# Attention megakernel on one core: first two units load their queries once and copy them on chip, and the weights are quantised in the bias stage

## The reference, cut to what matters

```python
q = heads(x @ Wq + bq); k = heads(x @ Wk + bk); v = heads(x @ Wv + bv)      # 48 x 1024 x 16
attn = einsum('bqd,bkd->bqk', q, k) / sqrt(HD)
rel_bias_h = einsum('bhwc,hkc->bhwk', rq, Rh)                                # q times a table of rows
rel_bias_w = einsum('bhwc,wkc->bhwk', rq, Rw)                                # q times a table of columns
attn = softmax(attn + rel_bias_h[..., None] + rel_bias_w[..., None, :])
x = x + einsum('bqk,bkd->bqd', attn, v) @ Wp + bp
wq1 = round(clip(w1 / alpha_w1, -8, 7)); wq2 = round(clip(w2 / alpha_w2, -8, 7))
x = x + ffn(layernorm(x), wq1, wq2)
```

## Time and profile before

| | us |
|---|---|
| median of 3 runs | 881.89 |
| lowest, highest | 879.38, 884.87 |
| the profiled execution | 880.72 |
| its span (first to last instruction of the program) | 878.9 |
| projection stage | 0 to 101.8 |
| bias stage | 101.8 to 159.4 |
| attention stage | 159.4 to about 762 |
| feed-forward stage | to 878.9 |

### The profile page before, as it was taken

The page is one execution under the profiler, slowest core; times in us unless marked ns, Lnnn a source line. Parts: engine busy times, 40 slices in busy tenths (PEclk is TensorE's granted clock), DMA queues, the critical chain, the costliest instruction groups (busy, mean ns, idle before and its releaser), DMA issues. The chain is left out here.

```text
span 878.9 us, 14775 instructions
## 1 busy us (share of the span) xinstructions
PE 775.8 (88%) x5656; PEld 404.5 (46%) x5656; DVE 696.7 (79%) x965; ACT 574.0 (65%) x969; POOL 447.7 (51%) x284
## 2 busy tenths in 40 slices
PE   4999456588999999999999999999999998678874
PEld 2655456243444444444444444444444441356653
DVE  6998844696888888888888888888888880179995
ACT  1343335136787778787878777787777878257673
POOL 3677796445373738474665748373734444012120
PEclk9999767679999999999999999999999999889986
DMA  7675599999977584939293949577690001333411
GB/s 195 214 223 192 177 286 363 311 184 184 155 151 163 123 186 95 203 76 213 69 209 68 222 82 201 107 158 151 132 178 13 13 1 34 116 132 102 145 37 54
DMA packets 65750, 130.02 MB, mean 148 GB/s; under 512 B 9535, under 2 KB 45392, under 8 KB 57224
## 3 DMA queue, kind: packets, MB, share of 16 engines
q1 hardware_dynamic: 57648, 115.95, 57.1%
q10 hardware_dynamic: 8032, 13.13, 4.3%
HBM read 89.73 MB, written 34.60 MB: 141 GB/s over the span
## 5 line engine op out<-in xcount | busy, mean ns | idle before, releaser
L1031 DVE TENSOR_REDUCE at_neg_max<-at_r_ps 128x1 f16<-128x1024 f32 x384 | 451.7, 1218 | 86.4 <-PE at_r_ps L903 86.4
L989 ACT ACTIVATE at_probs<-at_s_ps 128x512 f32<-128x512 f32 x768 | 410.8, 600 | 97.4 <-PE at_s_ps L923 96.5
L923 PE MATMUL at_s_ps<-op_mix_q,op_mix_k 128*128 128x512 f16 x768 | 264.3, 383 | 10.8 <-issue 3.9
L903 PE MATMUL at_r_ps<-op_mix_k,op_mix_q 128*128 128x256 f16 (+1 forms) x1920 | 239.9, 258 | 13.3 <-DMA op_mix_q<-bias_parts 8.6
L935 PE MATMUL at_o_ps<-at_probs,op_v_u 128*32 128x512 f32 x1536 | 204.1, 604 | 0.0
L903 PEld LDWEIGHTS at_r_ps<-op_mix_k,op_mix_q 128*128 128x128 f16 x1920 | 157.3, 100 | 91.3 <-DVE at_neg_max L1031 15.7
L822 POOL COPY op_mix_q<-op_mix_q 2x4096 f16<-2x4096 f16 x48 | 171.6, 3601 | 1.5
L923 PEld LDWEIGHTS at_s_ps<-op_mix_q,op_mix_k 128*128 128x128 f16 x768 | 73.8, 97 | 175.5 <-issue 74.4
L220 POOL MEMSET op_mix_q<- 2x10240 f32 x12 | 103.5, 8628 | 21.2 <-PE at_o_ps L935 21.1
L826 POOL TENSOR_TENSOR at_o_sb<-at_o_sb,at_inv_rows 128x512 f32<-128x512 f32 x24 | 30.7, 1279 | 141.1 <-DVE at_inv_rows L1047 139.9
L819 POOL COPY op_mix_q<-op_mix_q 2x1024 f16<-2x1024 f16 x24 | 24.9, 1036 | 113.0 <-ACT op_mix_q L994 113.0
(11 more groups left out here) (116 smaller groups left out, 655.2 us busy)
## 6 DMA issues: line engine op xcount, KB each, us to landing
op_mix_q<-qk_parts SPq DMA_DIRECT2D x48, 640.0 KB, 10.7
op_mix_q<-bias_parts SPq DMA_DIRECT2D x120, 120.0 KB, 9.6
op_mix_q<-bias_parts SPq DMA_DIRECT2D x72, 128.0 KB, 9.5
qk_parts<-op_mix_q SPq DMA_DIRECT2D x24, 256.0 KB, 2.4
v_rows<-pr_v_st SPq DMA_DIRECT2D x8, 768.0 KB, 4.1
op_mix_k<-qk_parts SPq DMA_DIRECT2D x48, 128.0 KB, 13.2
op_v_u<-v_rows SPq DMA_DIRECT2D x12, 512.0 KB, 13.9
op_mix_q<-bias_parts SPq DMA_DIRECT2D x24, 256.0 KB, 9.9
```

Of the source, the lines that this page charges most:

```text
L903: last = pe.matmul(r_ps[count % RRING][:, first // GROUP, first % GROUP:first % GROUP + n], mix_q[owner.buf][:, variant, j, qt * P:(qt + 1 ...
L923: pe.matmul(s_ps[use % SRING][:, :], mix_k[unit.buf][:, j, keys], mix_q[unit.buf][:, ops.VARIANT_OF[kt], j, queries], start=True, stop=Tru ...
L989: act.activation(probs[n % PRING][:, j, :], s_ps[use % SRING][:, :], ACT.Exp).then_inc(s_taken, 1)
L1031: dve.tensor_reduce(neg_max[half][:, j // 2, t, j % 2:j % 2 + 1], r_ps[count % RRING][:, :, :].rearrange("p h t -> p (h t)"), AX_X, ALU.ma ...
```

## The change

Four edits.

1. Units 0 and 1 load their queries into variant 0 alone (`load_first_q`, 4 DMAs of 128 KB each, with a semaphore `q_in` of their own). Variants 1 to 4 are made by copies of 64 partitions x 4096 float16. For unit 0 DVE makes them in the bias stage, two after item 3 and two after item 4. For unit 1 ACT makes two and POOL makes two at the start of the attention stage. All later units load as before (`load_q`).
2. The weights are quantised by DVE in the bias stage, w1 after item 0 and w2 after item 1.
3. SP asks for unit 0's first loads without waiting for `tab_lo`; the waits for `tab_lo` and for the quantised weights now stand ahead of `load_bias`.
4. POOL turns the queries half by half over the images, and PE waits for a half instead of the whole.

```diff
-        for r, part in enumerate((0, 0, 1, 1)):
-            src = q_or_k(0, part).unsqueeze(1).to_broadcast([HD, self.VARIANTS, QUAD * SEQ])
...
+    def load_first_q(self, sp, i):
+
+        for r, part in enumerate((0, 0, 1, 1)):
+            sp.dma_start(self.mix_q[i][r:self.A_AT:4, 0, :, :].rearrange("p j t -> p (j t)"), self.q_or_k(0, i, 0, part)).then_inc(self.q_in[i], 16)
+
+    def variant_of_q(self, i, variant):
+        return self.mix_q[i][0:self.A_AT, variant, :, :].rearrange("p j t -> p (j t)")
...
-                if g.last:
-                    prepare.quantise(dve, 0)
-                    prepare.quantise(dve, 1)
...
+    QUANTISE_AFTER, SPREAD_AFTER = (0, 1), {3: (1, 2), 4: (3, 4)}
...
-                for image in range(BATCH):
-                    for half in range(2):
+                for half in range(2):
+                    for image in range(BATCH):
...
-            sp.wait_ge(tables.tab_lo, 2 * CHUNKS)
-            ops.load_qkv(sp, 0, 0)
-            ops.load_hot(sp, hot_a, hot_b, parity)
+            ops.load_first_q(sp, 0)
+            ops.load_kv(sp, 0, 0)
+            ops.load_hot(sp, hot_a, hot_b, parity)
+            sp.wait_ge(prepare.quantised, 2)
+            sp.wait_ge(tables.tab_lo, 2 * CHUNKS)
...
-                if t == 1:
-                    pe.wait_ge(q_turned, (quad + 1) * 2 * BATCH)
+                    if t == 1 and ch * PER % BLK == 0:
+                        pe.wait_ge(q_turned, (quad * 2 + ch * PER // BLK + 1) * BATCH)
...
+                if i in QUANTISE_AFTER:
+                    prep.quantise(dve, QUANTISE_AFTER.index(i))
+                if i in SPREAD_AFTER:
+                    dve.wait_ge(ops.q_in[0], 16 * 4)
+                    dve.wait_ge(prep.quantised, 2)
+                    dve.wait_ge(tables.tab_lo, 2 * CHUNKS)
+                    for variant in SPREAD_AFTER[i]:
+                        dve.tensor_copy(ops.variant_of_q(0, variant), ops.variant_of_q(0, 0)).then_inc(ops.q_spread[0], 1)
...
+            pool.wait_ge(ops.q_in[1], 16 * 4)
+            for variant in Q_BY_POOL:
+                pool.tensor_copy(ops.variant_of_q(1, variant), ops.variant_of_q(1, 0)).then_inc(ops.q_spread[1], 1)
...
+            act.wait_ge(ops.q_in[1], 16 * 4)
+            for variant in Q_BY_ACT:
+                act.activation(ops.variant_of_q(1, variant), ops.variant_of_q(1, 0), ACT.Copy).then_inc(ops.q_spread[1], 1)
```

More of the change, by code:

```diff
@@ L155, in __init__ @@
         self.loaded = [self.sem(f"loaded{i}") for i in range(3)]
+        self.q_in, self.q_spread = ([self.sem(f"{n}{i}") for i in range(2)] for n in ("q_in", "q_spread"))
         early, late = (m[:, :, :, :].rearrange("p v j t -> p (v j t)") for m in self.mix_q[1:])
@@ L220, in zero_max, with load_kv, loads_of, q_or_k @@
         pool.memset(rows, 0.0).then_inc(self.max_zeroed, 1)
[L222 to L227, removed]
-        for r, part in enumerate((0, 0, 1, 1)):
-            src = q_or_k(0, part).unsqueeze(1).to_broadcast([HD, self.VARIANTS, QUAD * SEQ])
-            sp.dma_start(self.mix_q[i][r:self.A_AT:4, :, :, :].rearrange("p v j t -> p v (j t)"), src).then_inc(self.loaded[i], 16)
+    def load_kv(self, sp, image, i):
         for r, part in enumerate((0, 1, 0, 1)):
-            sp.dma_start(self.mix_k[i][r:self.A_AT:4, :, :].rearrange("p j t -> p (j t)"), q_or_k(1, part)).then_inc(self.loaded[i], 16)
+            sp.dma_start(self.mix_k[i][r:self.A_AT:4, :, :].rearrange("p j t -> p (j t)"), self.q_or_k(image, i, 1, part)).then_inc(self.loaded[i], 16)
         sp.dma_start(self.v_u[i][:, :, :, :].rearrange("p k h e -> p k (h e)"),
                      self.v_dram[bass.ds(image, 1), :, :, i * QUAD * SLOT:(i + 1) * QUAD * SLOT].rearrange("b p k e -> (b p) k e")).then_inc(self.loaded[i], 16)
+    def loads_of(self, buf, images):
+        return 16 * (self.N_LOADS * images - (4 if buf < 2 else 0))
+    def load_first_q(self, sp, i):
[3 more added lines that the diff above has]
+        return self.mix_q[i][0:self.A_AT, variant, :, :].rearrange("p j t -> p (j t)")
+    def q_or_k(self, image, i, which, part):
+        chunk, half = ((which, i), (2, which))[i == 2]
+        src = self.qk_dram[bass.ds(image, 1), chunk, part, half * QC:(half + 1) * QC, :]
+        return src.rearrange("b (d j) t -> (b d) (j t)", d=HD)
+    def load_q(self, sp, image, i):
+        for r, part in enumerate((0, 0, 1, 1)):
+            src = self.q_or_k(image, i, 0, part).unsqueeze(1).to_broadcast([HD, self.VARIANTS, QUAD * SEQ])
+            sp.dma_start(self.mix_q[i][r:self.A_AT:4, :, :, :].rearrange("p v j t -> p v (j t)"), src).then_inc(self.loaded[i], 16)
     def load_bias(self, sp, u, i):
@@ L738, in phase_attention @@
     SRING, RRING = 3, 2
+    Q_BY_ACT, Q_BY_POOL = (1, 2), (3, 4)
     with Phase(nc, "at") as ph:
@@ L741, in phase_attention @@
         MAX_ROW, TILE_ORDER = ops.MAX_ROW, ops.TILE_ORDER
[L742 removed]
+        consts, loaded = ops.consts, ops.loaded
         neg_max = [ph.sb(f"neg_max{h}", [P, QUAD // 2, TILES, 2], F16) for h in range(2)]
@@ L863, in _ @@
             ops.copy_hot(sp)
-            ops.load_qkv(sp, 0, 1)
+            ops.load_first_q(sp, 1)
+            ops.load_kv(sp, 0, 1)
             sp.wait_ge(ops.bias_stored[2], 32)
@@ L876, in emit @@
                     need(sp, pv_done, unit.u * STEPS)
-                    ops.load_qkv(sp, nxt.image, nxt.buf)
+                    ops.load_q(sp, nxt.image, nxt.buf)
+                    ops.load_kv(sp, nxt.image, nxt.buf)
                 if not unit.first:
@@ L941, in _ @@
             pe.wait_ge(ops.hot_out, 16 * ops.N_HOT)
-            pe.wait_ge(loaded[0], 16 * N_LOADS)
+            pe.wait_ge(loaded[0], ops.loads_of(0, 1))
+            pe.wait_ge(ops.q_spread[0], ops.VARIANTS - 1)
             for n in range(STEPS):
@@ L959, in emit @@
                     if ROWS in todo:
-                        pe.wait_ge(loaded[nxt.buf], (nxt.turn + 1) * (16 * N_LOADS))
+                        pe.wait_ge(loaded[nxt.buf], ops.loads_of(nxt.buf, nxt.turn + 1))
+                        if nxt.u == 1:
+                            pe.wait_ge(ops.q_spread[1], ops.VARIANTS - 1)
                         pe.wait_ge(ops.max_zeroed, nxt.u + 1)
```

## The result

| | before | after |
|---|---|---|
| median of 20 runs, us | 882.69 | 877.65 |
| lowest, highest | 876.91, 888.62 | 870.05, 880.51 |
| the profiled execution | 880.72 | 879.21 |
| its span | 878.9 | 877.0 |
| first row of the attention stage | 163.72 | 167.67 |

The ratio is 0.9921, with a 95% interval of 0.9898 to 0.9944: 7 us faster by the ratio, 5.0 us by the medians, under 1% either way. The forecast was 2.0 us slower (883.9). The median lies in the range given, 872 to 889, but the sign is wrong.

The account below looks back on a forecast made before the run. PE bounds the attention stage, a PE-ACT-DVE chain through three PSUM buffers the bias stage. Removals give -10.1 us, the longer bias stage +12.1: +2.0 on the profiled 880.72 is 882.7, or 883.9 on the median's scale; range 872 to 889.

Parts of the forecast that it names:

- length of the bias stage: Bias stage: it would last 69.7 instead of 57.6 us, +12.1 us.
- unit 1's wait: Attention stage: PE's 3.90 us wait at the step that needs unit 1 would go.
- the order at the pair: Bias stage, before item 4: POOL reaches its memset before DVE reaches its first copies, within 0 to 3 us; chance 0.72.
- The pair behind the memset: Bias stage: DVE's first two copies wait out POOL's 8.63 us memset, one span of 8 to 11 us.
- the first rival: Bias stage: the memset does not hold DVE, or DVE reaches its pair first; total 873 us, chance 0.22.
- How late POOL is: Bias stage: quantising delays POOL by 6.4 of its 6.8 us, so the memset starts at r 43.0.
- Quantising beside POOL: Bias stage: each DVE instruction pays one POOL operation, adding 5.5 us for w1 and 4.2 for w2.
- Half by half: Bias stage: PE starting after four copies instead of eight gains 0; if it were the limit, up to 2 us.
- the border: Between projection and bias stages: without quantising there, the bias stage starts at about 99.85, 2.0 us gained.
- the copy: Bias stage: one DVE copy of 4096 elements for unit 0 takes 1.23 us, at most 2.7.
- unit 1's copies: Attention stage start: ACT's and POOL's copies lie beside other work, price 0; ACT at worst 0.4 us late.
- the slow rival: Attention stage: POOL's two copies for unit 1 take up to 10 us each and are the bound; 892 us, chance 0.06.

Follow-up runs that it names:

- h3: The changed kernel, unedited, one profiled execution: 872.49 us, with DVE's first pair of copies taking 3.35 us.
- g2: The changed kernel run again unedited, nine times: six from 870.03 to 872.2 us, three from 877.38 to 878.63; the profiled one was upper.
- h1: The changed kernel, unedited, one profiled execution: 880.27 us, with DVE's first pair of copies taking 11.20 us.
- f4: e3 with the queries turned in the old order and PE waiting for all eight copies: 874.3 us.
- f2: The kernel before, changed only so that unit 1 loads its queries once and ACT and POOL copy them: 874.38 us, ratio 0.9921.
- e1: The changed kernel with POOL's memset of unit 0 waiting until DVE's first pair of copies is done: 871.5 us.
- f3: e3 with unit 1's queries loaded five times again and no copies for it: 881.91 us, ratio 0.9993.
- e3: The changed kernel with POOL's memset moved between the turning of the second and third head groups: 871.39 us.
- g1: Early memset, quantising in the projection stage, and unit 0's copies after items 4 and 5 instead of 3 and 4: 871.28 us.

## Why the forecast was wrong

The terms of the sum beside what two executions of the changed kernel show, one of each group, in us against the profiled run of before:

| term | forecast | profiled run (upper) | h3 (lower) |
|---|---|---|---|
| start of the bias stage | -2.0 | -1.2 | -1.1 |
| length of the bias stage | +12.1 | +9.0 | +1.4 |
| from the attention stage's start to the first row | -4.2 | -3.9 | -3.9 |
| first row to the turn of step 5 (unit 1's wait) | -3.9 | -5.9 | -6.5 |
| sum | +2.0 | -1.9 | -10.2 |

Two steps failed. One is the order at the pair: "I have them within 0 to 3 us, POOL ahead" holds for no trace, and half of the executions escape the memset. The other is the size of two terms, and it alone turns the sign, since the upper group, where the mechanism of the forecast is at work, is faster than before too (median 879.21 against 882.69).

- **The pair behind the memset.** Mechanism right, in every upper execution that has a trace: forecast 11 us from DVE's arrival to its end, measured 11.2 to 11.9. The order had 0.72: DVE came 0.65 us ahead of the memset in the profiled run, 1.2 us in g2, and was held there only because POOL's last turning copy stood before it. The case of the first rival came true in 9 of 20 executions (16 of 32 with g2 and h1 to h3), by the way named there last (DVE first), not by a memset that doesn't hold. Memsets do hold: L751 at 9.73, L1187 at 1.08. It had 0.22. With the Trainium skill's rule (SBUF — State Buffer, section "Who interferes with whom"), that the second to issue blocks, this trace agrees: 9.73 us for a copy of 1.21 behind a memset, which only writes. The second half of the rule, that whoever issues first has it, agrees with what makes the two groups.
- **How late POOL is.** The forecast had POOL later "by some 6.4 of the 6.8 us" of quantising, and so the memset at r 43.0. It began at r 40.1, 3.7 later than before (36.5): 1.5 from w1 and 2.1 from w2. That is 2.9 us earlier than forecast, and what stands behind it in the upper group is earlier by about as much: item 4 ends at 56.4 where the forecast had 59.0. This is the 3 us by which +12.1 was too much.
- **Quantising beside POOL.** Waits put at 5.5 + 4.2 us, measured 2.8 + 2.4. The model "Each instruction of a chain then pays one POOL operation" is an upper end: the first of a chain starts at once, and while a DVE instruction waits, POOL's runs anyway and is not added. Item 2 ended at 31.9 where the forecast had 35.7, item 3 at 39.6 where it had 43 to 46.
- **Half by half put at 0**, "if it were the limit, up to 2 us". PE had waited 5.6 us for POOL in the bias stage (3.9 at item 1, 1.7 at item 3), a row that the forecast did not use; 1.5 are left. f4 shows 2.8 us for it where the memset is early. f1, with halves and without quantising, ends item 3 at 33.9 where before had 38.7 (f2: 38.0); how much of that is the halves and how much the next term no run separates.
- **A term that was not in the sum:** ACT's issue of the stores behind item 2 went from 4.08 to 0.95 us. The two kernels whose unit 0 loads five times (before, f2) have 4.1 and 3.4 there, fourteen executions of the others 0.9 to 1.8 and one (e1) 3.0. That fewer bytes in flight shorten it fits these numbers; no run isolates it.
- **The gain behind unit 1's wait** was undersized. From the first row to the turn of step 5 it went from 47.40 to 41.53 us: 5.9, where the forecast counted the 3.90 of the wait. f3 shows the same 2 us as matmuls at a lower granted clock behind the wait (0.59 over 5 us, 0.71 before, 1.00 in e3).
- **The number of the first rival was luck in part.** Its 873 is near the lower group (median 870.8), but its own terms, a pair of 2.5 and low parts of 4.88 us behind r 43 to 46, give the end of item 4 at 50.4 to 53.4 and not at "48 to 50", which would be 876 to 879 by the rest of its sum. h3 has item 4 at 47.8, because item 3 had ended at 38.9.
- **Right:** the border in its direction (1.2 us in the profiled run, 1.1 to 2.4 over all, forecast 2.0); the copy (1.21 us, forecast 1.23); both DMA waits gone; unit 1's copies hidden but for ACT's. These take 3.6 us each on both engines, so the slow rival falls. ACT's maxima begin 1.8 us behind PE's turn at 188.17, before 1.05, that is 0.8 us late where 0.4 was the worst, since the queries landed at + 15.5 and not + 14.5. The second pair is free in upper executions (2.34 us in a gap), but takes 5.28 us in h3, where it meets the memset.

The best kernel here is f1 (g4 is the same one again): memset early, quantising in the projection stage, the rest of the change as it is. g4's six runs lie within 870.02 and 871.44, ratio 0.9877 (0.9854 to 0.9901); g1 does not differ from it. The changed kernel beside it has a median of 870.64 but reaches 878.63.

## What to carry to other kernels

Where a VectorE copy and a long GpSimd instruction both come due at about the same time, find out which asks first and by how much; if it is within a microsecond, the kernel can have two times, as here, and one semaphore or another place for the long instruction settled it. A change that takes bytes out of the queues should be costed at every wait that ends on a transfer and at every engine that issues transfers, and an idle TensorE costs more than the gap. Look at the sorted times, not only at their median.

## What was not expected of the hardware

- VectorE and GpSimd took turns instruction by instruction: a copy of 1.21 us took 9.73 behind a memset of 8.63, and the memset 9.59 behind a copy. Arithmetic with one operand in PSUM (L742) was not held: six of the short pieces take 3.66 us at 151.48, with POOL idle, and 3.66 in h3 at 142.89, beside the memset.
- Five matmuls took 1.06 us instead of 0.60 behind a wait of 6.56 us, where the granted clock was 0.59 over 5 us; before, behind a wait of 3.90 us, also 1.06, with 0.71.
- One chunk at 1.82 or 1.89 instead of 1.07 us, by the clock, goes with the group that is 8 us slower in three of four traces of it; the fourth (g2) had 1.07.
